# First attention on full-height operands, its maxima sent by DMA, and inputs loaded in two parts

## The chip, the cores and the metric

One NeuronCore of a Trainium2 chip runs the whole program. TensorE (PE) multiplies matrices into PSUM, VectorE (DVE), ScalarE (ACT) and GpSimd (POOL) do the elementwise work, SyncE (SP) issues the DMA transfers. The engines run in parallel, each in its own program order, and wait for each other by semaphores. The metric is the device time of one execution in microseconds (us).

## The reference

A two-layer transformer decoder over 32 sequences of 128 tokens, width 128. Each layer has a cross attention (queries from the layer-normed x, keys and values from a context) and a mixture-of-experts feed-forward block, each added to x. The changed part is the attention of layer 0, with 16 heads of 8 dimensions:

```python
qh = (q @ Wq.T + bq).reshape(B, S, H, Hd).transpose(0, 2, 1, 3)   # H = 16, Hd = 8, S = 128
kh = (k @ Wk.T + bk).reshape(B, S, H, Hd).transpose(0, 2, 1, 3)
vh = (v @ Wv.T + bv).reshape(B, S, H, Hd).transpose(0, 2, 1, 3)
attn = jax.nn.softmax(jnp.einsum('bhqd,bhkd->bhqk', qh, kh) / jnp.sqrt(jnp.float32(Hd)), axis=-1)
out = jnp.einsum('bhqk,bhkd->bhqd', attn, vh)
return out.transpose(0, 2, 1, 3).reshape(B, S, D) @ Wo.T + bo
```

## The kernel before

The program is a sequence of blocks with a barrier between them: loading of the inputs (L1401 to L1427), of a selection constant (L1388 to L1397), of the layer-0 weights (`layer0_weights`, L963), then the attention of layer 0 (`attention0`, L599), the feed-forward block of layer 0 (`ffn`, L1005), the attention of layer 1 (`attention`, L68, with heads of 64 dimensions) and its feed-forward block.

`attention0` handles the 32 sequences in 8 groups of 4. A group's projections are five fills of one PSUM bank (`F_BANK`): x transposed, context transposed, queries, keys, values. Each fill goes PE, ACT (upper part), DVE (the remainder, "lower part"), and the next fill waits for that DVE instruction. Precision is kept by splitting each number into an upper and a lower f16 part. A head's scores need four products over 8 dimensions (upper and lower of q times upper and lower of k), so its operands are laid out over 32 partitions: SP writes the split q and k to a scratch tensor in DRAM (L645) and reads them back spread out (L652, four transfers of 32 partitions each for q and four for k). Partition block 32i to 32i+31 then holds head i of four, and the index r of 0 to 3 selects one of four such sets.

The loop runs over steps s = -11 to 67. A sequence b has two steps, 2b and 2b+1, each with 8 heads. In step s PE does, in this order (L752 to L769): `scores(s)`; `values(s-2)` if s is odd; the transpose of the row maxima of sequence (s+LM0-2)/2 if s is even; `maxima(s+LM0)`; the output projection of sequence (s-4)/2 if s is even; a fill; `values(s-2)` if s is even; the transpose of the attention result if s is odd. LM0 is 4. `maxima` multiplies q by k once so that DVE can take each row's maximum (L856). The maxima, negated, are transposed (L693), copied by ACT (L814), and added into the scores by a second matmul with a selection matrix (L671). So `scores` is 8 matmuls of q and k (L667) and 8 of the selection (L671), each on 32 of the 128 rows of the array and 128 columns long, issued as pairs in two different row blocks. `maxima` is 8 such matmuls (L685). ACT then takes the exponential twice, once to f32 and once to f16 (L807, L808), POOL subtracts the two for the lower part (L916), and `values` is 24 matmuls, 9 columns each (L709 to L711).

What waits for what around the change: `maxima` of a group's first step waits for its q and k transfers (L679); `scores` waits for the copied maxima (L660) and for the exponentials two steps back; the exponentials wait for POOL two steps back; `values` waits for POOL and, at a sequence's first step, for the addition into x (L702). In the fill of group g the steps are 8g-11 to 8g-7.

Of the kernel before, what the change touches and what calls it, by code (L numbers as in the profile page):

```python
# [8 lines left out]
F32 = mybir.dt.float32  # L9
F32R = mybir.dt.float32r  # L10
F16 = mybir.dt.float16
# [5 lines left out]
P = 128  # L17
# [565 lines left out]
LM0 = 4  # L583
RING0 = 4


def fill_of(s):

    g, at = divmod(s + 11, 8)
    if at < 5 and 0 <= g < G:  # L590
        return g, at
    return None


def fills_before(s):
    return sum(1 for t in range(-11, s) if fill_of(t))


def attention0(nc, mem, psum, x_all, ctx_all, const, w, dram):  # L599

    NP = 2 * B
    FIRST, LAST = -11, NP + 4
# [9 lines left out]
    ident, sel = const["ident"], const["sel0"]  # L612
# [6 lines left out]
    q_x, k_x = sb("q_x", [P, 2, 4, 512], F16), sb("k_x", [P, 2, 4, 512], F16)  # L619
    v_hi, v_lo = sb("v_hi", [P, 2, GB, H, D0 + 1], F16), sb("v_lo", [P, 2, GB, H, D0 + 1], F16)  # L620
    negmax, negmax_t = sb("negmax", [P, 2, P]), sb("negmax_t", [P, 2, P], F16)
# [3 lines left out]

    T_BANK, M_BANK, PV, F_BANK = psum[:, 0:4, :], psum[:, 4:6, :], psum[:, 6, :], psum[:, 7, :]
# [4 lines left out]
    s_spill, s_spread = sem("spill"), sem("spread")  # L631
# [4 lines left out]
    with nc.Block() as block:  # L636

        @block.sync
        def _(sp):
            for g in range(G):  # L640
                for m, (hl, wide) in enumerate(((q_hl, q_x), (k_hl, k_x))):
                    sp.wait_ge(s_lo, 5 * g + 3 + m)
                    if g:
                        sp.wait_ge(s_spread, 128 * g)
                    sp.dma_start(dram[m, g % 2], hl[:, :, :]).then_inc(s_spill, 16)  # L645
                    sp.wait_ge(s_spill, 32 * g + 16 * m + 16)
                    if g >= 2:
                        sp.wait_ge(s_sc, 8 * (g - 2) + 8)
                    for t in range(4):
                        part = t // 2 if m == 0 else t % 2  # L650
                        src = dram[m, g % 2].rearrange("(r p) l n -> l p r n", p=32)[part]
                        sp.dma_start(wide[t::4, g % 2, :, :], src).then_inc(s_spread, 16)  # L652

        @block.tensor
        def _(pe):
            def scores(s):
                b, j = divmod(s, 2)
                tok = slice(b % GB * P, (b % GB + 1) * P)
                par = b // GB % 2
# [3 lines left out]
                for r in range(4):  # L663
                    for i in (2 * j, 2 * j + 1):
                        rows = slice(32 * i, 32 * i + 32)
                        o = T_BANK[:, 2 * (s % 2) + i % 2, r * P:(r + 1) * P]
                        nc.tensor.matmul(o, k_x[rows, par, r, tok], q_x[rows, par, r, tok], start=True, stop=False)  # L667
                    for i in (2 * j, 2 * j + 1):
                        rows = slice(32 * i, 32 * i + 32)
                        o = T_BANK[:, 2 * (s % 2) + i % 2, r * P:(r + 1) * P]  # L670
                        last_ = nc.tensor.matmul(o, sel[rows, r, :], negmax_t[rows, b % 2, :], start=False, stop=True)  # L671
                last_.then_inc(s_sc, 1)

            def maxima(s):
                b, j = divmod(s, 2)
                tok = slice(b % GB * P, (b % GB + 1) * P)
                par = b // GB % 2
# [4 lines left out]
                for r in range(4):  # L682
                    for i in (2 * j, 2 * j + 1):
                        rows = slice(32 * i, 32 * i + 32)
                        last_ = nc.tensor.matmul(M_BANK[:, i % 2, r * P:(r + 1) * P], q_x[rows, par, r, tok],  # L685
                                                 k_x[rows, par, r, tok], start=True, stop=True)
                last_.then_inc(s_mm, 1)

            def transpose_maxima(b, s):
                pe.wait_ge(s_max, 2 * b + 2)  # L690
                if n := fills_before(s):
                    pe.wait_ge(s_lo, n)
                nc.tensor.transpose(F_BANK[:, 0:P], negmax[:, b % 2, :], ident[:]).then_inc(s_nmt_mm, 1)  # L693

            def values(s):
                b, j = divmod(s, 2)
                par = b // GB % 2
# [5 lines left out]
                for r in range(4):  # L703
                    for i in (2 * j, 2 * j + 1):
                        h = 4 * r + i
                        o = PV[:, h * (D0 + 1):(h + 1) * (D0 + 1)]
                        q = slice((4 * (i % 2) + r) * P, (4 * (i % 2) + r + 1) * P)
# [15 lines left out]
            def fill(s):  # L723
# [7 lines left out]
                if kind == 0:  # L731
                    pe.wait_ge(s_xhat, g + 1)
                if kind < 2:
# [38 lines left out]
        def _(act):  # L772
            def fill(s):
# [5 lines left out]
                elif kind < 4:  # L779
                    if g:  # L780
                        act.wait_ge(s_spill, 32 * (g - 1) + 16 * (kind - 1))
                    m = kind - 2
                    nc.scalar.activation((q_hl, k_hl)[m][:, 0, :], F_BANK, ACT.Identity,
                                         bias=w["bias"][:, m:m + 1]).then_inc(s_hi, 1)
                else:
                    if g >= 2:
                        act.wait_ge(s_pv, 8 * (g - 2) + 8)
                    nc.scalar.activation(v_hi[:, g % 2, :, :, 0:D0].rearrange("p j h d -> p (j h) d"),
# [3 lines left out]
            for s in range(FIRST, LAST):  # L792
# [16 lines left out]
                if even and 0 <= s + LM0 - 2 < NP:  # L809
                    b = (s + LM0 - 2) // 2  # L810
                    act.wait_ge(s_nmt_mm, b + 1)
                    if b >= 2:
                        act.wait_ge(s_sc, 2 * b - 2)
                    nc.scalar.activation(negmax_t[:, b % 2, :], F_BANK[:, 0:P], ACT.Copy, bias=lifted).then_inc(s_nmt, 1)  # L814
# [4 lines left out]
        def _(dve):  # L819
            def statistics(g):  # L820
                for t in range(GB):
# [9 lines left out]
            def lower(s):  # L831
# [11 lines left out]
                else:  # L843
                    last_ = nc.vector.tensor_tensor(
                        v_lo[:, g % 2, :, :, 0:D0].rearrange("p j h d -> p (j h) d"),
                        F_BANK.rearrange("p (h d) -> p h d", d=D0),
                        v_hi[:, g % 2, :, :, 0:D0].rearrange("p j h d -> p (j h) d"), ALU.subtract)
                last_.then_inc(s_lo, 1)

            def maxima(s):  # L850
                b, j = divmod(s, 2)
                dve.wait_ge(s_mm, s + 1)
                if j == 0 and b >= 2:
                    dve.wait_ge(s_nmt_mm, b - 1)
                out = negmax[:, b % 2, 64 * j:64 * j + 64].rearrange("p (i n) -> p i n", n=32)[:, :, 0:4]
                nc.vector.tensor_reduce(out, M_BANK.rearrange("p i (r k) -> p i r k", k=P), AX.X, ALU.max,  # L856
                                        negate=True).then_inc(s_max, 1)
# [17 lines left out]
            nc.vector.memset(negmax[:, :, :], 0.0)  # L875
# [4 lines left out]
            for s in range(FIRST, LAST):  # L880
# [9 lines left out]
                if s % 8 == 2 and (s + 14) // 8 < G:  # L890
                    statistics((s + 14) // 8)

        @block.gpsimd
        def _(pool):
# [14 lines left out]

            normal(0)  # L910
            for s in range(FIRST, LAST):
                if s % 8 == 3 and (s + 13) // 8 < G:
                    normal((s + 13) // 8)
# [49 lines left out]
def layer0_weights(nc, mem, bank, const, d, w, raw):  # L963


    s_raw, s_mm, s_hi, s_lo = (mem.enter_context(nc.semaphore(n)) for n in ("raw_in", "turned", "split_hi", "split_lo"))
    with nc.Block() as block:

        @block.sync
        def _(sp):  # L970
            for n in ("wq", "wk", "wv", "wo", "gate", "bv", "bo"):
                sp.dma_start(raw[n], d[n]).then_inc(s_raw, 16)
            sp.dma_start(w["bias"][:, 0:1], d["bq"]).then_inc(s_raw, 16)
            sp.dma_start(w["bias"][:, 1:2], d["bk"]).then_inc(s_raw, 16)
            sp.wait_ge(s_raw, 16 * 9)
# [583 lines left out]
```

## Time and profile before

| | us |
|---|---|
| median of 3 runs | 1698.66 (1693.28 to 1699.65) |
| the profiled execution | 1695.49 |
| its span, first to last instruction | 1693.7 |
| first scores of layer 0 to its last exponentials | 71.1 to 335.4 |
| PE busy over the span | 1401.0 (83%) |
| DVE, ACT, POOL busy | 949.1, 814.0, 661.4 |

The profile lists instructions with start and duration. "L685" is line 685 of the kernel. PE is the matmul, PEld the load of its stationary operand, SPq the issue of a DMA by SP. A bracket such as [6.15 <-DMA k_x_a<-spill] says how long the engine had been idle and what released it. PEclk is the granted TensorE clock as a share of 2.4 GHz.

### The profile page before, as it was taken

To read this page: it belongs to the slowest core of one execution; us is meant where nothing else is said; L and a number is where in the kernel's file an instruction comes from. 1 tells how busy PE (TensorE), PEld (TensorE's weight loads), DVE (VectorE), ACT (ScalarE), POOL (GpSimd) and SP (SyncE) were. 2 spreads that over 40 slices of the span, in tenths; PEclk is the share of its full clock that TensorE was granted. 3 is DMA by queue.
4 is the path that set the end of the run, shared out by engine and by line. 5 is a ranking of instruction groups with operands and counts; after the bars stand their busy time and mean duration, and the time that the engine had idled before them with its cause. 6 is when DMAs were issued, how large, how long until landed. Compare 5 with 4: busy or idle time off the path is not lost. (4 is left out here: it accounts for less than half of the span.)

```text
span 1693.7 us, 31779 instructions
## 1 busy us (share of the span) xinstructions
PE 1401.0 (83%) x11720; PEld 1123.0 (66%) x11720; DVE 949.1 (56%) x2066; ACT 814.0 (48%) x1335; POOL 661.4 (39%) x556
## 2 busy tenths in 40 slices
PE   0599999806599999999993798988988989836698
PEld 0477777606488888888882477777777777736486
DVE  0455544337656665666563666665666666527665
ACT  0255655521344444444442465655656556521354
POOL 1266656602155555555552123333232332412254
PEclk9999655555799999999996899998999899965799
DMA  4211111040000000000001000000000000010000
GB/s 114 75 39 39 46 63 45 2 149 1 1 1 1 1 1 1 0 0 0 0 0 62 1 2 1 2 1 3 2 1 3 2 1 2 2 32 1 1 25 25
DMA packets 27575, 31.59 MB, mean 19 GB/s; under 512 B 4721, under 2 KB 21682, under 8 KB 27314
## 3 DMA queue, kind: packets, MB, share of 16 engines
q1 hardware_dynamic: 27442, 29.75, 5.7%
q8 instruction: 91, 1.49, 0.4%
q14 instruction: 42, 0.34, 0.1%
HBM read 23.45 MB, written 6.29 MB: 18 GB/s over the span
## 5 line engine op out<-in xcount | busy, mean ns | idle before, releaser
L1347 POOL TENSOR_TENSOR w_lo_f<-weighted_f,w_hi_f 128x512 fp32r<-128x512 f32 x232 | 300.6, 1296 | 345.8 <-ACT w_hi_f L1289 345.8
L565 POOL TENSOR_TENSOR p_lo_l<-probs_l,p_hi_l 128x512 f16<-128x512 f32 x128 | 148.2, 1158 | 336.5 <-ACT p_hi_l L358 336.5
L1327 DVE TENSOR_TENSOR hidden_f<-psum,gate_act_f 128x512 f32<-128x512 f32 x232 | 160.5, 692 | 210.0 <-PE psum L1239 199.3
L1304 ACT ACTIVATE gate_act_f<-psum 128x512 f32<-128x512 f32 x232 | 138.7, 598 | 269.0 <-PE psum L1239 267.6
L916 POOL TENSOR_TENSOR p_lo_a<-probs_a,p_hi_a 128x1024 f16<-128x1024 f32 x64 | 135.9, 2127 | 112.9 <-ACT p_hi_a L808 112.9
L1333 DVE TENSOR_TENSOR weighted_f<-psum,hidden_f 128x512 f32<-128x512 f32 x232 | 160.5, 692 | 9.0
L1239 PE MATMUL psum<-x_lo_f,w_hi 128*128 (+1 forms) x384 | 153.8, 401 | 0.0
L1237 PE MATMUL psum<-x_hi_f,w_hi 128*128 (+1 forms) x384 | 152.0, 396 | 1.8 <-PEq L1135 1.8
L1238 PE MATMUL psum<-x_hi_f,w_lo 128*128 (+1 forms) x384 | 151.8, 395 | 0.0
L1289 ACT ACTIVATE w_hi_f<-weighted_f 128x512 fp32r<-128x512 f32 x232 | 144.9, 625 | 2.2 <-DVE weighted_f L1333 2.2
L356 ACT ACTIVATE probs_l<-psum,lift_l 128x512 f32<-128x512 f32 x128 | 88.0, 688 | 105.0 <-PE psum L232 105.0
L228 PE MATMUL psum<-q_a_l,k_a_l 64*128 64x128 f16 x512 | 115.9, 226 | 19.2 <-ACT negmax_t_l L350 11.8
L232 PE MATMUL psum<-negmax_t_l,sel 64*128 64x128 f16 x512 | 115.4, 225 | 0.0
L230 PE MATMUL psum<-q_a_l,k_b_l 64*128 64x128 f16 x512 | 115.4, 225 | 0.0
L229 PE MATMUL psum<-q_b_l,k_a_l 64*128 64x128 f16 x512 | 115.4, 225 | 0.0
L856 DVE TENSOR_REDUCE negmax_a<-psum 128x8 f32<-128x1024 f32 x64 | 78.3, 1224 | 42.6 <-PE psum L685 42.6
L807 ACT ACTIVATE probs_a<-psum 128x1024 f32<-128x1024 f32 x64 | 65.5, 1023 | 68.9 <-PE psum L671 68.9
L1243 PE MATMUL psum<-comb_t_f,pick 128*128 (+1 forms) x232 | 92.2, 397 | 0.0
L459 DVE TENSOR_REDUCE negmax_l<-psum 128x4 f32<-128x512 f32 x128 | 87.0, 682 | 1.6 <-PE psum L202 1.3
L358 ACT ACTIVATE p_hi_l<-psum,lift_l 128x512 f16<-128x512 f32 x128 | 87.0, 679 | 0.0
L1237 PEld LDWEIGHTS psum<-x_hi_f,w_hi 128*128 128x128 f32 x384 | 73.3, 191 | 19.1 <-issue 2.2
L1238 PEld LDWEIGHTS psum<-x_hi_f,w_lo 128*128 128x128 f32 x384 | 72.6, 189 | 17.4
(257 smaller groups left out, 3797.9 us busy)
## 6 DMA issues: line engine op xcount, KB each, us to landing
q_x_a<-spill SPq DMA_DIRECT2D x32, 128.0 KB, 2.6
k_x_a<-spill SPq DMA_DIRECT2D x32, 128.0 KB, 2.5
spill<-q_hl_a SPq DMA_DIRECT2D x8, 256.0 KB, 2.0
spill<-k_hl_a SPq DMA_DIRECT2D x8, 256.0 KB, 2.9
out<-x_all SPq DMA_DIRECT2D x8, 256.0 KB, 2.3
pick_raw<-c_pick SPq DMA_DIRECT2D x1, 1536.0 KB, 6.2
stage<-L_ffn_w SPq DMA_DIRECT2D x3, 256.0 KB, 3.0
stage<-L_xattn_Wq SPq DMA_DIRECT2D x1, 512.0 KB, 3.5
```

Of the source, the lines that this page charges most:

```text
L228: nc.tensor.matmul(o, ka, qa, start=True, stop=False)
L229: nc.tensor.matmul(o, ka, q_b[rows, parity, ch, tok], start=False, stop=False)
L565: nc.gpsimd.tensor_tensor(p_lo[:, r, :], probs[:, r, :], p_hi[:, r, :], ALU.subtract).then_inc(s_exp_lo, 1)
L916: nc.gpsimd.tensor_tensor(p_lo[:, s % RING0, :], probs[:, s % 2, :], p_hi[:, s % RING0, :], ALU.subtract).then_inc(s_plo, 1)
L1237: nc.tensor.matmul(dst[:, :], hi[:, a], x1, start=True, stop=False)
L1238: nc.tensor.matmul(dst[:, :], lo[:, a], x1, start=False, stop=False)
L1239: nc.tensor.matmul(dst[:, :], hi[:, a], x2, start=False, stop=True).then_inc(done, 1)
L1289: nc.scalar.activation(w_hi[:, slot, :], weighted[:, (parity * nc_ + k) % 2, :], ACT.Copy).then_inc(s_wh, 1)
L1304: nc.scalar.activation(gate_act[:, slot, :], GATE[slot][:, :], ACT.Silu).then_inc(s_silu, 1)
L1327: nc.vector.tensor_tensor(hidden[:, slot, :], UP[slot][:, :], gate_act[:, slot, :], ALU.mult).then_inc(s_hid, 1)
L1333: nc.vector.tensor_tensor(weighted[:, slot, :], CB[slot][:, :], hidden[:, slot, :], ALU.mult).then_inc(s_a, 1)
L1347: nc.gpsimd.tensor_tensor(w_lo[:, slot, :], weighted[:, (parity * nc_ + k) % 2, :], w_hi[:, slot, :].bitcast(F32), ALU.subtract).then_inc( ...
```

## The change

Operands of `attention0` now take all 128 rows of the array. q is spread into `q_pad`, where head i of a set has data only in partitions 32i to 32i+31 of its own 512 columns and zeros elsewhere, so one matmul of 128 rows and 512 columns gives four heads (`scores`: 2 matmuls a step in place of 16), and `maxima` is 8 matmuls of 128 rows. Partition 3 of k holds ones, and partition 3 of q the negated maxima of the sequence, written by one more DMA per sequence (`maxima_row`); the selection constant, its block and its matmuls go. The q transfers are eight of 16 partitions and one that clears partition 3; the k transfers are three of 32 partitions and one of 31. There are three buffers in place of two, LM0 is 6, the fills of group g are at steps 8g-14 to 8g-10, and `scores` waits for the DMA of the maxima. DVE and POOL set `q_pad` and `k_x` at the start of the attention block. SP follows the step order. The opening loads the first group's rows of x, the weights and the first group's rows of the context first, and the other rows last, in the same block; the statistics and the context transpose of group 1 wait for them.

```diff
-LM0 = 4
+LM0 = 6
+FILL0 = 14
+NB0 = 3
+SPREADS = 13
@@ SP
-            for g in range(G):
-                for m, (hl, wide) in enumerate(((q_hl, q_x), (k_hl, k_x))):
-                    sp.wait_ge(s_lo, 5 * g + 3 + m)
...
-                    for t in range(4):
-                        sp.dma_start(wide[t::4, g % 2, :, :], src).then_inc(s_spread, 16)
+            def spread_queries(g):
+                sp.wait_ge(s_spill_q, 16 * g + 16)
+                if g >= NB0:
+                    sp.wait_ge(s_sc, 8 * (g - NB0) + 8)
+                halves = narrow_q[g % 2].rearrange("(r i d) l n -> i (d l) r n", r=4, i=4)
+                for i in range(4):
+                    for t in range(2):
+                        sp.dma_start(q_pad[32 * i + t:32 * i + 32:2, g % NB0, :, i, :], halves[i]).then_inc(s_spread, 16)
+                others = q_pad[3:4, g % NB0, :, 1:4, :].rearrange("o r i n -> o r (i n)")
+                sp.dma_start(others, nothing[:, :].unsqueeze(1).broadcast_to([1, 4, 1536])).then_inc(s_spread, 16)
+            def spread_keys(g):
+                sp.wait_ge(s_spill_k, 16 * g + 16)
+                halves = narrow_k[g % 2].rearrange("(r p) l n -> l p r n", p=32)
+                for t in range(4):
+                    skip = int(t == 3)
+                    sp.dma_start(k_x[t + 4 * skip::4, g % NB0, :, :], halves[t % 2, skip:32]).then_inc(s_spread, 16)
+            def maxima_row(b):
+                sp.wait_ge(s_nmt, b + 1)
+                tok = slice(b % GB * P, (b % GB + 1) * P)
+                dst = q_pad[3:4, b // GB % NB0, :, :, tok].rearrange("o r i n -> o (r i) n")
+                sp.dma_start(dst, negmax_t[:, b % 4, :]).then_inc(s_row[b % 4], 16)
+            sp.wait_ge(s_clear, 3)
+            for s in range(FIRST, LAST):
+                if s % 2 == 0 and 0 <= s + LM0 - 2 < NP:
+                    maxima_row((s + LM0 - 2) // 2)
+                g, at = divmod(s + FILL0, 8)
+                if at == 3 and 0 <= g < G:
+                    spill_queries(g)
+                if at == 4 and 0 <= g < G:
+                    spill_keys(g)
+                if at == 5 and 0 <= g < G:
+                    spread_queries(g)
+                if at == 6 and 0 <= g < G:
+                    spread_keys(g)
@@ PE, scores
-                pe.wait_ge(s_nmt, b + 1)
+                pe.wait_ge(s_row[b % 4], 16 * (b // 4 + 1))
...
+                for r in (2 * j, 2 * j + 1):
+                    last_ = nc.tensor.matmul(T_BANK[:, 2 * (s % 2) + r % 2, :], k_x[:, par, r, tok], q_pad[:, par, r, :, tok],
+                                             start=True, stop=True)
@@ PE, maxima
-                    pe.wait_ge(s_spread, 128 * (s // 8) + 128)
+                    pe.wait_ge(s_spread, SPREADS * 16 * (s // 8 + 1))
...
+                for r in (2 * j, 2 * j + 1):
+                    for i in range(4):
+                        last_ = nc.tensor.matmul(M_BANK[:, r % 2, i * P:(i + 1) * P], q_pad[:, par, r, i, tok],
+                                                 k_x[:, par, r, tok], start=True, stop=True)
@@ DVE and POOL, at the start of the block
-            nc.vector.memset(negmax[:, :, :], 0.0)
+            nc.vector.memset(nothing[:, :], 0.0)
+            nc.vector.memset(k_x[:, :, :, :], 1.0)
+            nc.vector.memset(q_pad[:, 0, :, :, :], 0.0).then_inc(s_clear, 1)
...
+            nc.gpsimd.memset(q_pad[:, 1, :, :, :], 0.0).then_inc(s_clear, 1)
+            nc.gpsimd.memset(q_pad[:, 2, :, :, :], 0.0).then_inc(s_clear, 1)
@@ the opening block
+                sp.dma_start(rows(x_all, 0, GB), x_rows[:, 0:GB, :]).then_inc(s_in, 16)
...
+                    sp.dma_start(dst, src).then_inc(s_raw, 16)
+                for dst, src in ((rows(ctx_all, 0, GB), ctx_rows[:, 0:GB, :]), (maskt[:, :], a["mask_BxS2_fk1"]),
...
+                sp.dma_start(rows(x_all, GB, B), x_rows[:, GB:B, :]).then_inc(const["s_rest"], 16)
+                sp.dma_start(rows(ctx_all, GB, B), ctx_rows[:, GB:B, :]).then_inc(const["s_rest"], 16)
```

## Rows read from the trace of the kernel before

**Rows 1.** Stretches: us, busy time and count per engine, PEclk, DMA share.
```profile
71.00:107.00 36.00, 32.14 (x407) 24.47 (x406) 17.87 (x31) 22.71 (x32) 21.41 (x15) 1.00 0.16 53
182.50:247.20 64.70, 60.29 (x788) 46.30 (x788) 32.44 (x63) 37.54 (x55) 41.81 (x28) 0.50 0.12 39
1180.00:1500.00 320.00, 291.64 (x3331) 238.95 (x3331) 194.84 (x474) 190.36 (x321) 98.46 (x96) 0.94 0.01 2
```

**Rows 2.** PE in order of time, layer 0: start, us, line, shape, count.
```profile
62.92 0.61 PE L685 MATMUL psum<-k_x_a,q_x_a 32*128 32x128 f16 x8 [1.32 <-DVE negmax_a L856]
...
177.88 0.63 PE L741 MATMUL psum<-c_lo_a,wk_hi 128*128 128x512 f32 x1
178.31 0.63 PE L742 MATMUL psum<-c_hi_a,wk_lo 128*128 128x512 f32 x1
...
180.74 0.40 PE L685 MATMUL psum<-k_x_a,q_x_a 32*128 32x128 f16 x8
```

**Rows 3.** ACT in order of time: exponentials of steps 0, 16, 24, 32, 54, 56, 63.
```profile
72.17 1.02 ACT L807 ACTIVATE probs_a<-psum 128x1024 f32<-128x1024 f32 x1 [0.28 <-PE psum L671]
...
139.95 1.02 ACT L807 ACTIVATE probs_a<-psum 128x1024 f32<-128x1024 f32 x1 [0.33 <-PE psum L671]
175.06 1.02 ACT L807 ACTIVATE probs_a<-psum 128x1024 f32<-128x1024 f32 x1 [0.33 <-PE psum L671]
208.30 1.02 ACT L807 ACTIVATE probs_a<-psum 128x1024 f32<-128x1024 f32 x1 [0.33 <-PE psum L671]
...
302.18 1.02 ACT L807 ACTIVATE probs_a<-psum 128x1024 f32<-128x1024 f32 x1 [0.69 <-PE psum L671]
309.37 1.02 ACT L807 ACTIVATE probs_a<-psum 128x1024 f32<-128x1024 f32 x1 [0.70 <-PE psum L671]
333.44 1.02 ACT L807 ACTIVATE probs_a<-psum 128x1024 f32<-128x1024 f32 x1 [1.43 <-PE psum L671]
```

**Rows 4.** PE in order of time, one step's scores in layer 0.
```profile
305.84 0.32 PE L667 MATMUL psum<-q_x_a,k_x_a 32*128 32x128 f16 x2
305.94 0.32 PE L671 MATMUL psum<-negmax_t_a,sel 32*128 32x128 f16 x2
```

**Rows 5.** PE in order of time, scores in layer 1.
```profile
1018.05 0.22 PE L228 MATMUL psum<-q_a_l,k_a_l 64*128 64x128 f16 x1
1018.10 0.22 PE L229 MATMUL psum<-q_b_l,k_a_l 64*128 64x128 f16 x1
```

**Rows 6.** SP's key transfers, then the DMA view of 182 to 190 us.
```profile
183.28 2.53 SPq L652 DMA_DIRECT2D k_x_a<-spill  x4
...
q1 hardware_dynamic: 651, 0.64, 24.6%
...
k_x_a<-spill SPq DMA_DIRECT2D x4, 128.0 KB, 2.6
```

**Rows 7.** The opening and the first group, in order of time.
```profile
4.29 4.74 SPq L1411 DMA_DIRECT2D ctx_all<-ctx  x1
...
20.80 0.36 SPq L1392 DMA_DIRECT2D sel_raw<-c_sel  x1
...
29.87 0.48 PE L983 MATMUL psum<-ident,raw_wq 128*128 128x128 f32 x1 [9.55 <-DMA bias<-L_xattn_bk]
...
33.08 0.27 DVE L875 MEMSET negmax_a<- 128x256 f32 x1 [0.39 <-PEq L967]
...
40.47 1.12 PE L736 MATMUL psum<-ident,xhat_a 128*128 128x128 f32 x4 [8.09 <-POOL xhat_a L906]
...
51.21 0.75 DVE L841 SCALAR_TENSOR_TENSOR k_hl_a<-psum,bias,k_hl_a 128x512 f16<-128x512 f32 x1 [2.46 <-ACT k_hl_a L783]
...
60.99 0.61 PE L685 MATMUL psum<-k_x_a,q_x_a 32*128 32x128 f16 x8 [6.15 <-DMA k_x_a<-spill]
```

**Rows 8.** Groups by line: xcount, busy us, mean ns, idle before.
```profile
L1150 DVE MEMSET comb_t_f<- 32x4096 f32 x2 | 6.9, 3472 | 1.8 <-issue 1.8
L916 POOL TENSOR_TENSOR p_lo_a<-probs_a,p_hi_a 128x1024 f16<-128x1024 f32 x63 | 133.8, 2127 | 111.7 <-ACT p_hi_a L808 111.6
```

More of the change, by code:

```diff
@@ L595, in fills_before @@
 def fills_before(s):
-    return sum(1 for t in range(-11, s) if fill_of(t))
+    return sum(1 for t in range(-FILL0, s) if fill_of(t))
 def attention0(nc, mem, psum, x_all, ctx_all, const, w, dram):
     NP = 2 * B
-    FIRST, LAST = -11, NP + 4
+    FIRST, LAST = -FILL0, NP + 4
     scale = float(np.float32(1.0) / np.sqrt(np.float32(D0)))
@@ L630, in attention0 @@
     s_fill, s_hi, s_lo = sem("fill"), sem("hi"), sem("lo")
-    s_spill, s_spread = sem("spill"), sem("spread")
+    s_spill_q, s_spill_k, s_spread = sem("spill_q"), sem("spill_k"), sem("spread")
+    s_row = [sem(f"row_{n}") for n in range(4)]
+    s_clear = sem("clear")
     s_mm, s_max, s_nmt_mm, s_nmt = sem("max_mm"), sem("max"), sem("nmt_mm"), sem("nmt")
@@ L658, in scores @@
                 tok = slice(b % GB * P, (b % GB + 1) * P)
-                par = b // GB % 2
-                pe.wait_ge(s_nmt, b + 1)
+                par = b // GB % NB0
+                pe.wait_ge(s_row[b % 4], 16 * (b // 4 + 1))
                 if s >= 2:
                     pe.wait_ge(s_exp_hi, s - 1)
[L663 to L671, printed above, removed]
+                for r in (2 * j, 2 * j + 1):
+                    last_ = nc.tensor.matmul(T_BANK[:, 2 * (s % 2) + r % 2, :], k_x[:, par, r, tok], q_pad[:, par, r, :, tok],
+                                             start=True, stop=True)
                 last_.then_inc(s_sc, 1)
@@ L676, in maxima @@
                 tok = slice(b % GB * P, (b % GB + 1) * P)
-                par = b // GB % 2
+                par = b // GB % NB0
                 if s % 8 == 0:
-                    pe.wait_ge(s_spread, 128 * (s // 8) + 128)
+                    pe.wait_ge(s_spread, SPREADS * 16 * (s // 8 + 1))
                 if s >= 1:
                     pe.wait_ge(s_max, s)
[L682 to L686, printed above, removed]
+                for r in (2 * j, 2 * j + 1):
+                    for i in range(4):
+                        last_ = nc.tensor.matmul(M_BANK[:, r % 2, i * P:(i + 1) * P], q_pad[:, par, r, i, tok],
+                                                 k_x[:, par, r, tok], start=True, stop=True)
                 last_.then_inc(s_mm, 1)
@@ L732, in fill @@
                     pe.wait_ge(s_xhat, g + 1)
+                if kind == 1 and g == 1:
+                    pe.wait_ge(const["s_rest"], 32)
                 if kind < 2:
@@ L889, in _ @@
                     lower(s)
-                if s % 8 == 2 and (s + 14) // 8 < G:
-                    statistics((s + 14) // 8)
+                if s % 8 == 7 and (s + 17) // 8 < G:
+                    statistics((s + 17) // 8)
         @block.gpsimd
@@ L1524, in constants @@
     rows = np.arange(P)
-    sel0 = np.zeros((P, 4, P), f)
     sel1 = np.zeros((P, 8, P), f)
-    for m in range(4):
-        sel0[rows % 32 == m, m, :] = 1
     for m in range(8):
@@ L1554 @@
     out = nc.dram_tensor("out", (B, S, D), F32, kind="ExternalOutput").ap()
[L1555 removed]
+    spill = (nc.dram_tensor("narrow_q", (2, P, 2, 512), F16, kind="Internal").ap(),
+             nc.dram_tensor("narrow_k", (2, P, 2, 512), F16, kind="Internal").ap())
     program(nc, args, out, spill)
```

135 lines of the change are left out of this document (62 added, 73 removed).

## The prediction

> **What bounds the kernel now.** I read the stretches first. The change touches the first 335 us, so only the layer-0 attention and the opening matter. In its loop PE is busy 32.1 of 36 us and 60.3 of 64.7 us, while DVE, ACT and POOL are at about half to two thirds [rows 1]. PE sets the pace. Its clock comes next: PEclk is 0.50 in 182.5 to 247.2 us, the lower level (1.2 GHz). Up to about 179 us the column prints 1.00, but the instructions contradict it: eight maxima matmuls took 0.61 us at 62.9, and 0.40 at 180.7, in a short stretch that began right after two 512-column projections on all 128 rows [rows 2]. So the loop runs at 1.2 GHz nearly throughout. Layer 1's attention, on 64 rows and with wider fills, has 0.94 granted, which is the full level for 88% of its time [rows 1].
>
> The exponentials give the pace. Step 0 to step 63 lasts 72.17 to 333.44, 261.3 us. A pair of steps without a fill takes 309.37 - 302.18 = 7.19 us, so eight steps 28.8. Eight steps with fills take 175.06 - 139.95 = 35.1, so five fills add 6.3. The next eight, with the short stretch at full clock, took 33.2: about 3.4 us of full clock saved 1.9 us [rows 3].
>
> **The change in the loop.** At the low clock `scores` costs what it did. Now a pair of 32-row matmuls starts every 0.10 to 0.11 us, eight pairs are 0.85 us [rows 4]. Then two matmuls of 512 columns follow at 0.43 us (178.31 - 177.88), 0.86 [rows 2]. The selection matmuls were half of the pairs, and this is what pays for the lost pairing. `maxima` loses its pairing without such a saving: four starts of 0.107 become eight, +0.42 a step, +0.85 a pair. Of that 0.25 lies under DVE's normalisation, for which PE waits at the end of an odd step. So a pair goes from 7.19 to 7.8, eight steps to 31.2, with fills 37.5.
>
> At the full clock a 128-column matmul starts every 0.05 to 0.056 us [rows 5], and what streams halves: scores -0.86 a pair, maxima -0.8, projection and the two transposes -0.6 together (estimates from the same halving). `values` is bound by its 24 loads of the stationary operand and stays, as do the waits for DVE. A pair takes 5.6, eight steps 22.4, with fills (6.3 becomes 4) 26.4. As a check, this is a ratio of 1.4, and the stretch above ran 5.3 us of work in 3.4, 1.55. POOL needs 21.4 us in 36 us of the loop, ACT 22.7 [rows 1]; 22.4 to 26.4 lies just above, so these are the next bound.
>
> How much of the loop gets the full clock no row shows. The ends are none, as now, and 88% as in layer 1. Nearest is layer 1, since both now stream mostly over the array's height, but here PE stops twice a pair for DVE. I take two thirds. Rates then mix: with fills 1/(0.667/26.4 + 0.333/37.5) = 29.3, without 24.7. Fills of groups 2 to 7 lie in steps 0 to 47: 6 x 29.3 + 24.7 + (24.7 x 7/8 - 3 for six steps without maxima) = 219 us.
>
> The moved wait is `maxima` of a group's first step, now at step 8g-6, for 13 transfers. In front of it on SP, from the start T of step 8g-10: the copied maxima are ready at T+2.9, one row (0.5) and the spill of k (0.5), nine q transfers (at least 0.4 each with half the descriptors, at most 0.64; 4.4), the row of step 8g-8 at T+9.1, four k transfers in 2.53 [rows 6]. The last is issued at T+11.1 and lands 2.6 later [rows 6], T+13.7. PE comes to it at T+12.8 (four steps of 2.95, scores, a transpose). That is a wait of 1 us, seven times, 7. Behind it on PE stand the projection, the fill and `values`, so ACT and POOL run dry too, and nothing hides it. The rows of maxima themselves are issued four steps ahead of their use, over 11 us against some 3, and cost nothing even if one is held up by the q transfers. Loop: 219 + 7 - 261.3 = -35.3.
>
> The k transfer of 31 partitions has no row. If it goes like one of 32 it lands in 2.6. If its 31 x 4 pieces of 1 KB go one after another: 651 packets took 24.6% of 16 x 8 us, 48 ns each [rows 6], so 124 take 6.0 in place of 0.4, and it lands 5.6 later. The nearest row is that of 32 partitions; I take it in the sum, and the other end is a rival. On this the Trainium skill has a rule ("DMA: Bandwidth & Descriptors", section "Why a DMA increments its semaphore by 16 and not by 1"): a transfer runs on the largest number of engines up to 16 that divides its slowest dimension on both sides. By it 31 rows go to one engine, and the sum would be the rival's below. No row of this trace shows such a shape.
>
> **The opening.** SP ends the last issue at 9.03 (4.29 + 4.74). The new order puts eleven small issues of about 0.46 before it, so the block ends at about 14.4 rather than 20.8; the selection block (20.80 to 24) and the wait of the weights block (to 29.87) go, its work (29.87 to 33.08) and a barrier stay. The attention block starts at 18.0, not 33.1 [rows 7]. There the memsets stand ahead of the statistics: DVE has 1536 + 6144 + 8192 elements at 0.85 ns (3472 ns for 4096) [rows 8], 13.4 us. POOL has two of 8192, without a row: at DVE's rate 13.9, at 2.08 ns (2127 for 1024, two inputs) [rows 8] 34.1. I take 13.9, one output and no input being nearer to a memset; it runs beside DVE's and ends before the statistics do. With the 7.4 us from 33.08 to 40.47 and the dropped 0.3, the first transposes start at 38.5: -2.0 of the 15 that the loads give. The late rows of x and context are in SBUF before group 1 asks; if not, their wait is again behind the first group's keys. The Trainium skill ("VectorE: DVE Perf Modes", "Zero memsets can be issued as uint32 (trn2)") would halve the zero fill of `q_pad`, 3.5 us less on DVE; the 16-bit memsets of this trace are too small to tell.
>
> **The first group.** From its transposes to its first maxima now 60.99 - 40.47 = 20.5 [rows 7]; nine q transfers in front of the keys, instead of four, add 0.7, since the keys are spilled only after 51.96. From there to the first exponential 11.2 us now, with two steps of fills. With LM0 = 6 all five fills of group 1 come first: four of them lasted 40.47 to 51.96, 11.5, the fifth some 4, then two transposes and the last step, 2.2, and the row's DMA, 1: 18.7, +7.5. Sum +8.2.
>
> **Sum.** -35.3 - 2.0 + 8.2 = -29. The profiled execution took 1695.49 (span 1693.7 and 1.8 around it), 0.2% under the median of 1698.66; from it, 1666.
>
> **Rivals.** (a) The keys' last transfer goes piece by piece, and a wait takes the place of the pace. 5.6 us at each of the seven group changes and once in the first group: +45, 1711, slower than before. For it: 31 has no divisor. Against it: the step lengths hide it in part if the loop is slower than I think. It decides from 3.6 us of lateness on (8 x 3.6 = 29, the whole gain), and from 4.7 the loss is one that can be measured (29 and 8.5). (b) The clock stays at 1.2 GHz. Loop 6 x 37.5 + 31.2 + 24.3 = 280.5, four steps last longer than the transfers, so no wait: +19.2 - 2.0 + 8.2 = +25, 1721. For it: PE busy at 93% did not raise it so far [rows 1]. Against: the only rises in the loop came after full-height work. (c) The loop gains, but POOL fills its buffers at the higher price: transposes at 56.6 in place of 38.5, +18, 1684. (d) The change of operands doesn't pay at all because POOL and ACT take over as bound: that is the 22.4 of the forecast, it can't cost more.
>
> **How the numbers follow.** Forecast 0.42, (a) 0.33, (b) 0.15, (c) 0.10. Low end: full clock all the time, 6 x 26.4 + 22.4 + 16.6 = 197, no wait, halved zero fills: 1695.5 - 64 + 8.2 - 2.0 - 3.5 = 1634; high end: most of (b), 1720. The forecast's own range is 1634 to 1690. What a measurement can tell here is 0.5%, 8.5 us. Faster: 0.38 of the forecast's 0.42, 0.02 of (a), 0.05 of (c), 0.45. Slower: 0.24 of (a), 0.13 of (b), 0.01 of (c), 0.38. The rest, 0.17, is no change.
>
> **What would show it.** Right: PEclk at 1.00 in most of the loop, with eight maxima in under 0.7 us; an exponential pair every 5.6 us without fills; PE idle before a group's first maxima, released by `k_x`, about 1 us. The first transposes start near 38.5, the first exponential near 78. Wrong by (a): that wait is over 5 us and recurs in each group, and the 31-row transfer lands some 8 us after its issue. By (b): PEclk 0.50 and a pair at 7.8. By (c): POOL's memsets over 10 us each. The forecast fails altogether if SP's queue holds up the rows of maxima so that `scores` waits at every sequence.

## The result, and the profile after

The changed kernel takes 1708.75 us (median of 4 runs, 1707.64 to 1708.9), the kernel before 1697.94 beside it. The ratio is 1.0067, with a 95% interval of 1.0046 to 1.0087: slower by 0.7%. The interval lies above 1, but its lower end is just under the 0.5% that the prediction took as the least a measurement can tell from no change. The forecast was 1666, faster.

The stretches come first, as [rows 1] did. Columns as there.

```profile
71.00:107.00 36.00, 23.34 (x169) 16.68 (x169) 16.05 (x25) 13.98 (x21) 13.59 (x11) 0.62 0.14 45
182.50:247.20 64.70, 43.18 (x626) 33.27 (x627) 31.54 (x64) 34.94 (x53) 40.21 (x27) 0.82 0.15 47
1190.00:1510.00 320.00, 291.73 (x3339) 239.35 (x3336) 196.33 (x480) 191.15 (x322) 100.51 (x100) 0.94 0.01 2
```

The second row shows the odd thing about this result. PE's granted clock rose from 0.50 to 0.82, PE is busy 43.2 us of 64.7 instead of 60.3, and DVE, ACT and POOL do about as much in the stretch as before (31.5, 34.9 and 40.2 us against 32.4, 37.5 and 41.8). So the engine that set the pace got its relief, and the pace stayed. What took its place stands in the waits of PE between 60 and 360 us (total, how many, the longest):

```profile
PE psum L719 <- DMA k_x_a<-narrow_k: 62.0, 8, 13.5
PE psum L745 <- DVE x_all L914: 13.3, 13, 1.4
```

L719 are the maxima, and the wait is the moved one, for a group's key transfers. Before there was one such wait, of 6.2 us, the one in the last row of [rows 7]. Now there are eight: 13.5 us in the first group and 48.5 in the seven changes of group, 6.9 each on average. Over the whole loop PE is busy for 174.8 us of 260.8, against 241.4 of 261.3 before. This is the change to group 4, SP's queue first and then PE:

```profile
189.65 0.70 SPq L666 DMA_DIRECT2D q_pad_a<-nothing_a  x1
190.40 0.57 SPq L679 DMA_DIRECT2D q_pad_a<-negmax_t_a  x1
191.02 3.11 SPq L673 DMA_DIRECT2D k_x_a<-narrow_k  x4
```

```profile
191.71 1.01 PE L719 MATMUL psum<-k_x_a,q_pad_a 128*128 128x128 f16 x8
192.80 1.06 PE L705 MATMUL psum<-q_pad_a,k_x_a 128*128 128x512 f16 x2
194.04 0.38 PE L729 MATMUL psum<-ident,negmax_a 128*16 128x128 f32 x1 [0.18 <-DVE negmax_a L897]
201.44 1.04 PE L719 MATMUL psum<-k_x_a,q_pad_a 128*128 128x128 f16 x8 [7.02 <-DMA k_x_a<-narrow_k]
203.23 1.06 PE L774 MATMUL psum<-ident,xhat_a 128*128 128x128 f32 x4
204.77 0.59 PE L705 MATMUL psum<-q_pad_a,k_x_a 128*128 128x512 f16 x2
205.81 0.61 PE L719 MATMUL psum<-k_x_a,q_pad_a 128*128 128x128 f16 x8
```

SP has issued the last key transfer at 194.13 and PE gets on at 201.44, 7.3 us later; [rows 6] have 2.6 from issue to landing for one of 32 partitions. The view by stretches for the same gap says how the data travels:

```profile
195.50:201.20 5.70, 0.00 (x0) 0.00 (x0) 0.00 (x0) 2.08 (x3) 4.53 (x3) 0.50 0.07 21
```

A DMA share of 0.07 is what one engine of sixteen would give (1/16 = 0.06), and the data moves at 21 GB/s. The last transfer, 31 partitions of 4 KB, is 127 thousand bytes; at that rate it takes 6.0 us, the 6.0 that rival (a) had worked out from packets. The L705 and L719 rows of this gap also show the two levels of the clock: two 512-column matmuls take 1.06 or 0.59 us, eight of 128 columns 1.04 or 0.61.

The opening and the first group, against [rows 7] and the memset of [rows 8]:

```profile
9.49 4.51 SPq L1446 DMA_DIRECT2D ctx_all<-ctx  x1
...
18.25 0.70 DVE L916 MEMSET nothing_a<- 1x768 uint32 x1 [0.48 <-PEq L1012]
20.18 5.18 DVE L917 MEMSET k_x_a<- 128x6144 f16 x1 [1.23 <-issue]
26.16 3.47 DVE L918 MEMSET q_pad_a<- 128x4096 uint32 x1 [0.80 <-issue]
31.35 0.87 DVE L864 BATCH_NORM_STATS2 stats_a<-x_all 128x6 f32<-128x128 f32 x4
...
18.03 6.92 POOL L953 MEMSET q_pad_a<- 128x8192 f16 x1 [17.60 <-POOLq L1012]
24.89 6.93 POOL L954 MEMSET q_pad_a<- 128x8192 f16 x1
...
37.32 1.12 PE L774 MATMUL psum<-ident,xhat_a 128*128 128x128 f32 x4 [19.87 <-POOL xhat_a L949]
...
49.23 5.16 SPq L664 DMA_DIRECT2D q_pad_a<-narrow_q  x8
54.43 0.71 SPq L666 DMA_DIRECT2D q_pad_a<-nothing_a  x1
55.19 2.68 SPq L673 DMA_DIRECT2D k_x_a<-narrow_k  x4
...
65.20 1.03 PE L719 MATMUL psum<-k_x_a,q_pad_a 128*128 128x128 f16 x8 [13.51 <-DMA k_x_a<-narrow_k]
```

SP has issued the late rows by 14.0 us, the selection block and the wait behind it are gone, and the attention block starts at 18.0. Then DVE's statistics wait for its memsets until 31.35, and the first transposes for the statistics. In the last row PE has waited 13.51 us for the keys, 7.3 of them after SP's last issue ended at 57.87.

And the exponentials of steps 0, 16, 24 and 32, as in [rows 3]; the last is at 343.97:

```profile
83.20 1.02 ACT L847 ACTIVATE probs_a<-psum 128x1024 f32<-128x1024 f32 x1 [1.13 <-PE psum L705]
...
152.94 1.02 ACT L847 ACTIVATE probs_a<-psum 128x1024 f32<-128x1024 f32 x1
187.10 1.02 ACT L847 ACTIVATE probs_a<-psum 128x1024 f32<-128x1024 f32 x1
221.66 1.02 ACT L847 ACTIVATE probs_a<-psum 128x1024 f32<-128x1024 f32 x1
```

Eight steps take 34.2 and 34.6 us, each with a wait of about 7 for keys in it, against 35.1 and 33.2 before.

Where the 13.0 us of the spans (1706.7 - 1693.7) come from, in four parts:

| | before | after | difference | forecast |
|---|---|---|---|---|
| to the first transposes | 40.47 | 37.32 | -3.2 | -2.0 |
| from there to the first exponential | 31.7 | 45.9 | +14.2 | +8.2 |
| first to last exponential (the loop) | 261.3 | 260.8 | -0.5 | -35.3 |
| the rest of the span | 1360.3 | 1362.7 | +2.5 | 0 |

### The profile page after: what moved, and what is told of

It is laid out like the page before. It is cut to its first block and busy times, and to the rows that moved or that the text cites. A ratio compares the mean times of both kernels' runs of the same rounds, so it can differ in the third digit from the quotient of the medians.

```text
span 1706.7 us, 30035 instructions
## 1 busy us (share of the span) xinstructions
PE 1338.4 (78%) x10824; PEld 1072.0 (63%) x10824; DVE 956.2 (56%) x2068; ACT 808.2 (47%) x1334; POOL 675.7 (40%) x558
## 5 line engine op out<-in xcount | busy, mean ns | idle before, releaser
L719 PE MATMUL psum<-k_x_a,q_pad_a 128*128 128x128 f16 x512 | 48.5, 251 | 62.9 <-DMA k_x_a<-narrow_k 62.0
```

## The experiments

"Theory" is that the key transfer of 31 partitions goes over one DMA engine and turns the gain into a wait. All times are medians; the kernel before is 1697.5 to 1699.3 in the comparisons. "Loop" is first to last exponential, always of the one profiled execution, and so are the waits and the clock.

**e1_split: the last key transfer of the changed kernel in two pieces.**

```diff
-                for t in range(4):
-                    skip = int(t == 3)
-                    sp.dma_start(k_x[t + 4 * skip::4, ...], halves[t % 2, skip:32])
+                for t in range(3):
+                    sp.dma_start(k_x[t::4, ...], halves[t % 2])
+                sp.dma_start(k_x[7:68:4, ...], halves[1, 1:17])      # 16 partitions
+                sp.dma_start(k_x[71::4, ...], halves[1, 17:32])      # 15 partitions
```

> The changed kernel with the key transfer of 31 partitions cut into one of 16 and one of 15, nothing else. Theory (the 31-partition transfer goes piece by piece and is what PE waits for): it lands about 2.6 us after its issue like its neighbours, the wait before a group's first maxima falls from about 7 us to 1 or 2 and in the first group by about 5, so 35 to 45 us less than the changed kernel, 1664 to 1674. Rival (SP's long order, 13 issues and the rows of maxima between, makes every key transfer late): one more issue in that order, so the same or up to 5 us slower, 1709 to 1714.

Measured: 1675.67, ratio 0.9874 (0.9858 to 0.9891). One more DMA in each group, the same bytes, and the kernel is 33 us faster than the changed one. The first group and the waits of PE:

```profile
57.15 0.60 SPq L673 DMA_DIRECT2D k_x_a<-narrow_k  x1
57.80 0.92 SPq L674 DMA_DIRECT2D k_x_a<-narrow_k  x1
...
60.23 1.04 PE L720 MATMUL psum<-k_x_a,q_pad_a 128*128 128x128 f16 x8 [8.58 <-DMA k_x_a<-narrow_k]
```

```profile
PE psum L720 <- DMA k_x_a<-narrow_k: 23.8, 8, 8.6
```

The last piece lands 2.4 us after its issue begins. The waits of PE for keys fall by 38.2 us (62.0 - 23.8), the span by 35.8 (1706.7 - 1670.9). The first exponential is at 77.31 and the loop 232.5 us.

**e2_first: the 31-partition transfer is issued first of the four, not last.**

```diff
-                for t in range(4):
+                for t in (3, 0, 1, 2):
```

> The changed kernel with the 31-partition key transfer issued first of the four instead of last. Theory (piece by piece, some 8 us from issue to landing): it starts three issues or about 1.9 us earlier and the others land before it, so each of the eight waits shortens by 1.9 us: 15 us less, 1694. Rival (all key transfers are late by SP's order): their last landing is where it was, no change, 1709.

Measured: 1699.52, ratio 1.0004 (0.9985 to 1.0022): 9 us less than the changed kernel, between the theory's 15 and the rival's none. The wait in the first group is 12.3 us, all eight are 50.5. An earlier start takes 1.4 us off each wait ((62.0 - 50.5) / 8), and what stays is still twice the 23.8 of e1_split. So the length of this transfer is the main cause, and its place at the end of the queue a small part of the wait.

**e5_before31: the kernel before, its last key transfer as 1 + 31 partitions.**

```diff
-                        sp.dma_start(wide[t::4, g % 2, :, :], src).then_inc(s_spread, 16)
+                        if m == 1 and t == 3:      # keys, last transfer
+                            sp.dma_start(wide[3:4, ...], src[0:1])
+                            sp.dma_start(wide[7::4, ...], src[1:32])
+                        else: ...                  # as before
```

> The kernel before with its last key transfer (32 partitions) issued as one of 1 and one of 31 partitions. It measures the shape by itself. Theory (31 rows go piece by piece): the transfer of 31 lands about 8 us after its issue, the first group starts 6 us later, and in the loop, where PE comes 4 us after the landing (191.8 against 187.8), 2 us of each of seven are seen: 1698 + 6 + 15 = 1719, and at least 1708. Rival (31 rows spread like 32): one issue more, 1698 to 1700.

Measured: 1713.03, ratio 1.009 (1.0074 to 1.0107). The old kernel, with its 32-row tiles, loses through this alone as much as the change did (1.009 against 1.0067; the intervals overlap):

```profile
58.83 0.68 SPq L654 DMA_DIRECT2D k_x_a<-spill  x1
...
66.66 0.60 PE L689 MATMUL psum<-k_x_a,q_x_a 32*128 32x128 f16 x8 [11.80 <-DMA k_x_a<-spill]
```

Issue to use is 7.8 us. This is the price by itself, away from the rest of the change. It shows as a first exponential 5.7 us later (77.84) and as waits of 6.2 us in five of the seven changes of group, 1.2 each instead of the 2 in all seven that were expected. The loop grows by 9.7 us (271.0). The other 3.5 are about what two groups of the kernel before had saved by a stretch at the full clock (33.2 and 33.3 us instead of 35.1 for eight steps); here no eight steps take less than 35.1 up to step 48, and PE is busy for 4.0 us more with the same work (245.4 against 241.4).

**e7_before30: the same with 2 + 30 partitions.** The edit is that of e5_before31 with the cut after two rows.

> The kernel before, its last key transfer (32 partitions of 4 KB) issued as 2 and 30 partitions instead of one; e5_before31 did this with 1 and 31, which made its 31-partition transfer land 7.8 us after issue and the kernel 1713. Theory (the pieces of a transfer go over as many engines as divide its partitions' count, and 31 has no divisor in reach but 1): 30 has 15, so it lands about 3 us after issue, and the time is 1697 to 1702. Rival (any count of partitions that isn't a multiple of 16 is slow, or two issues in place of one are what cost): landing 6 us or more after issue, as in e5_before31, time 1708 to 1714.

Measured: 1699.31, ratio 1.0004 (0.9989 to 1.0019).

```profile
59.08 0.92 SPq L654 DMA_DIRECT2D k_x_a<-spill  x1
...
62.06 0.60 PE L689 MATMUL psum<-k_x_a,q_x_a 32*128 32x128 f16 x8 [6.96 <-DMA k_x_a<-spill]
```

30 partitions are in use 3.0 us after the issue began, 31 after 7.8. Two issues in place of one cost nothing that can be measured. That the count isn't a multiple of 16 costs nothing either. 31 is slow; it has no divisor between 2 and 16, while 30 has 15.

**e4_opening: the kernel before with the new opening only.** The opening's issues, its waits and the weights block are those of the change (see its diff); the layer-0 attention and the selection block stay.

> The kernel before with the new opening alone (first group's rows and weights first, the rest late; the selection constant's block stays). Theory (the loads give their whole gain where no memsets stand behind them): the attention block starts at 14.4 + 3.2 + 3.5 = 21.3 rather than 33.1, all that follows moves with it, 12 us less than before, 1686. Rival (the late rows of x and context hold up group 1, or the first group waits for its transfers): under 5 us gained.

Measured: 1694.06, ratio 0.9982 (0.9969 to 0.9995), 3 us less instead of the theory's 12. The first exponential is at 67.21, 5.0 us earlier than before. The rest of what the opening could give went here, and neither of the rival's two reasons was it:

```profile
14.47 5.63 SPq L1388 DMA_DIRECT2D sel_raw<-c_sel  x1
...
24.52 0.63 ACT L1393 ACTIVATE sel<-sel_raw 128x512 f16<-128x512 f32 x1 [8.77 <-DMA sel_raw<-c_sel]
```

The selection's small load stands behind the late rows of x and context: its issue takes 5.63 us instead of 0.36 [rows 7], and ACT and the weights behind it wait. In the full change this load is gone. In the profiled execution (1696.53, the slowest of the ten) the loop is 3.6 us longer (264.9 against 261.3): from step 8 to 48 every eight steps take 35.1 us, whereas before two of the five groups had a stretch at the full clock and took 33.2 and 33.3. This isn't shown to be an effect of the opening, since it differs between executions of one kernel. PEclk prints 1.00 throughout this loop, though its eight maxima matmuls take 0.60 us, the time of the lower level; the mean clock of the execution then prints as 0.94. Of the 19 executions of the kernel before that ran beside this one, six print 0.94; their median is 1699.9 us, that of the other 13 is 1696.85.

**e6_early: e1_split with the large memsets in the opening block.**

```diff
+            # opening block; q_pad, k_x and nothing are allocated there
+            nc.vector.memset(nothing[:, :], 0.0)
+            nc.vector.memset(k_x[:, :, :, :], 1.0)
+            nc.vector.memset(q_pad[:, 0, :, :, :], 0.0)
+            nc.gpsimd.memset(q_pad[:, 1, :, :, :], 0.0)
+            nc.gpsimd.memset(q_pad[:, 2, :, :, :], 0.0)
```

> The changed kernel with the last key transfer cut into 16 and 15 partitions (e1_split), and its large memsets (the ones of k_x, the zeros of q_pad, the clear row's zeros) moved from the head of layer 0 into the opening block, where VectorE and GpSimd wait for the first transfers. Theory (the head of layer 0 is the memsets: statistics on VectorE start at 31.4 behind them, and the first transposes at 37.3): the first transposes come at 24 to 27 us, the first exponential 10 to 12 us earlier than in e1_split (77.3), at 65 to 67, and the time is 1663 to 1666. Rival (the transposes' other need, the weights and the rest of the rows, or the key transfers behind a busy queue, comes just behind): the first exponential only 2 to 5 us earlier, time 1671 to 1674.

Measured: 1666.87, ratio 0.9814 (0.9798 to 0.9831); 8.8 us less than e1_split by the medians, 5.9 by the two profiled spans.

```profile
9.31 3.47 DVE L1461 MEMSET q_pad_a<- 128x4096 uint32 x1 [0.80 <-issue]
...
25.99 1.12 PE L772 MATMUL psum<-ident,xhat_a 128*128 128x128 f32 x4 [8.39 <-POOL xhat_a L944]
```

The first transposes come 11.3 us earlier, the first exponential 10.2 (67.1). So in the changed kernel the memsets, not the loads, ended the opening.

**e9_ahead: e6_early with a group's projections and transfers one step earlier.**

```diff
-FILL0 = 14
+FILL0 = 15
```

> e6_early with the projections, spills and spreads of a group one step earlier in the order (15 steps ahead of the first use of a group instead of 14). Theory (the 2.2 us that e1_split still waits at each of seven changes of group is a transfer that lands a little late, not a queue that is full): the key waits at the group changes go to nothing, 7 times 2.2 = 15 us less in the loop and as much less time than e6_early if the granted clock stays as it is, 10 to 15 us. Rival (TensorE then waits for the next thing, VectorE's maxima or the exponentials, or the clock falls): the key waits go but the loop gets under 5 us shorter. Second rival: the projections now stand on the steps of the maxima's transposes and share their bank, and the step gets longer: same as e6_early or slower.

Measured: 1663.31, ratio 0.98 (0.9768 to 0.9832), the fastest kernel of the study. But it is only 3.6 us under e6_early, and the intervals overlap. The waits of PE from 40 to 330 us, in which e6_early has 23.9 us for the keys:

```profile
PE psum L743 <- DVE x_all L912: 18.2, 21, 1.4
PE psum L772 <- POOL xhat_a L944: 15.3, 7, 7.3
...
PE psum L717 <- DMA k_x_a<-narrow_k: 0.2, 1, 0.2
```

The key waits are gone. In their place PE waits longer for the residual sum (18.2 instead of 12.9 us) and for the next group's normalised rows: 15.3 us, of which 7.3 stand before the loop, at the first projection of group 1, and 8 are new in the loop. The loop is 230.6 us, 3.8 shorter. PE is idle for 7.3 us less in it (47.9 against 55.3), but the same instructions keep it busy for 3.6 us more (182.7 against 179.1), with a mean granted clock of 0.78 in place of 0.80. The theory of a late transfer holds, its price does not: the first rival, that the next wait steps in or the clock falls, is the better account.

**e3_extra: the kernel before with two idle full-height matmuls a step.** What was left open is the clock: 0.50 before, 0.82 after.

```diff
             def scores(s):
                 ...
+                for r in (0, 1):
+                    nc.tensor.matmul(T_BANK[:, 2 * (s % 2) + r, :], k_x[:, par, r, tok], q_x[:, par, r, :], ...)
                 for r in range(4):
```

> The kernel before, its maxima and scores still in 32-row tiles, with two more matmuls in every step of layer 0: all 128 rows of k_x against 512 columns, into the bank that the step's scores then overwrite. They do no needed work (64 steps of two). Theory (the granted clock in layer 0 rises because full-height matmuls take the place of those in 32-row tiles, not because the work is less): the loop's granted clock rises from 0.50 to 0.7 or more somewhere in its length, and the added 0.86 us a step at 1.2 GHz is paid back by all of TensorE's work going faster: loop 225 to 262 us, time 1665 to 1700. Rival (the clock is set by something else, such as the order of the transfers or how long TensorE waits): the granted clock stays 0.50, the step grows from 4.15 to about 5.0 us, the loop from 261 to about 315, and the time is about 1750. Below nothing added (loop under 261 with more work done) only the theory is left.

Measured: 1737.68, ratio 1.0236 (1.0209 to 1.0263). In stretches of 40 us:

```profile
150.00:190.00 40.00, 38.52 (x435) 26.08 (x434) 16.70 (x32) 19.56 (x28) 20.35 (x14) 0.50 0.13 41
...
230.00:270.00 40.00, 36.64 (x472) 24.51 (x471) 19.05 (x35) 21.36 (x32) 23.41 (x15) 0.67 0.13 41
```

Neither side had it. The clock stays at its lower level most of the time, the loop grows by 42.3 us (303.6), and the theory's 1665 to 1700 is refuted for this addition. Where it rose (0.67) eight steps took 36.8 instead of 41.7 us, so the rival's 1750 is missed too.

**e11_more: the same addition, to the kernel whose matmuls are all full height (e6_early).**

```diff
+                    nc.tensor.matmul(T_BANK[:, 2 * (s % 2) + r % 2, :], q_pad[:, par, r, 0, tok], k_x[:, par, r, :], ...)
                     last_ = nc.tensor.matmul(T_BANK[:, 2 * (s % 2) + r % 2, :], k_x[...], q_pad[...], ...)
```

> e6_early with two more matmuls in every step of layer 0: q_pad on all 128 rows against 512 columns of k_x, into the bank that the step's scores then overwrite; no needed work. It is e3_extra's addition, made to the kernel in which all matmuls of the loop are full height. Theory left after e3_extra (the clock comes with the share of the loop's time in which TensorE streams columns over the whole array; e3_extra added too little to a loop whose other half stayed in 32-row tiles): the granted clock of the loop, 0.74 to 0.87 in e6_early, rises to 0.95 or more, the added work is paid for in part, and the loop (234.3 us) grows by 0 to 15: time 1665 to 1682. Rival (more work means no better clock; what counts is something else, such as its pauses): the granted clock stays at 0.75 to 0.87, each step grows by 0.43 to 0.86 us, the loop by 27 to 40: time 1694 to 1707.

Measured: 1670.58, ratio 0.9825 (0.9807 to 0.9844). One stretch of e6_early, then the same of e11_more:

```profile
150.00:190.00 40.00, 31.68 (x428) 23.66 (x425) 23.55 (x44) 26.74 (x41) 25.93 (x17) 0.87 0.19 60
```

```profile
150.00:190.00 40.00, 33.68 (x462) 24.15 (x459) 22.43 (x41) 25.34 (x39) 26.16 (x17) 0.96 0.18 56
```

The added work is 64 x 0.43 = 27.5 us at the full clock; the loop grows by 5.1 (239.5). But PE's idle time in the loop fell too, from 55.3 to 46.7 us, of which 4.0 are key waits, so a part of this is cover for waits and not the clock. (The next expectation puts that fall at 24 to 11; the 11 leaves out the first group's wait.)

**e12_both and e13_half: the addition (two or one a step) on e9_ahead, which has no key waits.**

> e9_ahead with e11_more's addition: two more full-height matmuls of 512 columns in every step of layer 0, no needed work. In e11_more the granted clock rose from 0.67 to 0.87 (stretches of 40 us) to 0.84 to 0.96 and the loop grew by 5 us for 27 us of added work. Theory (the clock is carried by full-height streaming, and pauses at group changes bring it down): with no key waits the clock is 0.95 or more throughout, the loop 225 to 236 us (e9_ahead 230.6), time 1656 to 1668. Rival (the gain of e11_more was the key waits that its longer steps covered, 24 us in e6_early and 11 in e11_more, not the clock): without waits to cover, the added work shows, loop 245 or more, time 1677 or more.

> As e12_both with one added matmul a step instead of two: 13.7 us of added work at the full clock. Theory: the clock lies between e9_ahead's (0.76 to 0.90) and e12_both's, the loop at or below e9_ahead's 230.6, time 1653 to 1664. Rival: each added matmul costs its time, loop 237 or more, time 1670 or more.

Measured: e12_both 1665.95, ratio 0.9829 (0.9795 to 0.9864), loop 231.9; e13_half 1666.56, ratio 0.9806 (0.9786 to 0.9827), loop 237.8. e9_ahead first, then e12_both:

```profile
230.00:270.00 40.00, 32.38 (x450) 24.33 (x451) 20.14 (x32) 25.26 (x38) 25.10 (x12) 0.80 0.14 42
```

```profile
230.00:270.00 40.00, 31.39 (x454) 22.46 (x451) 20.78 (x33) 26.17 (x39) 25.56 (x15) 1.00 0.16 48
```

With no key waits to cover, 27.5 us of work that nobody needs costs 1.3 us in the loop (2.6 by the medians). It doesn't go into the other waits either: PE's idle time in the loop doesn't fall (49.9 us against 47.9), and PE is busy no longer with 127 matmuls more (182.0 against 182.7), because nearly all else on it runs at the full level (mean clock 0.96 against 0.78). That is the clock's own worth. As a change it brings nothing: neither kernel is faster than e9_ahead. e13_half misses the theory's 1653 to 1664 by 2.6 us; its profiled execution is the slowest of its four (1671.06), with a loop as the rival had it, and its clock lies between (0.88 to 0.91 from 110 to 270 us), as the theory had it. How one added matmul a step divides between cost and gain stays open.

## Why the prediction was wrong

**The step that failed** is the landing of the keys' last transfer: "The nearest row is that of 32 partitions; I take it in the sum". It was taken as 2.6 us and is 7.8 (e5_before31). It was seen, priced and left as rival (a), with a chance of 0.33. The prediction's own working had both ends, and no row of the trace chose between them. The row nearest in size was the wrong one: 30 partitions take 3.0 us and 31 take 7.8, so what counts is not the number of partitions but what divides it. Here the Trainium skill had the answer, "DMA: Bandwidth & Descriptors", section "Why a DMA increments its semaphore by 16 and not by 1": a transfer uses the largest number of engines, up to 16, that divides its slowest dimension on both sides. The runs agree with it in all cases tried: 31 partitions take 7.8 us, at one engine's share in the changed kernel, 30 partitions 3.0, and 16 + 15 partitions 2.4. A rule that names the shape at hand should have outweighed a row with another shape.

**The price of (a)** was 5.6 us in each of eight places, 45 together. The 5.6 held: in the first group of the changed kernel the keys are in use at 65.20, some 8.0 us after the last issue began (about 57.2), in e1_split 2.4. The split begins its last issue 0.6 us later, though, so each of its waits is shorter by 4.8 us on average, 38.2 together, and the time by 33; a late start of a group is given back in part behind the wait. That the 1711 of rival (a) lies only 2 us from the measured 1708.75 is in part luck: its 45 was 12 more than the split gave back, and the 1666 that it was added to was 10 too low.

**The rest of the sum** is tested by e1_split, the kernel that the forecast described.

- The clock: "I take two thirds". In e1_split the granted clock from 90 to 290 us is 0.81, 0.91, 0.84, 0.73 and 0.79 in stretches of 40 us, a mean of 0.82, which is the full level for 63% of the time. Right, as a choice that no row had supported.
- The loop: 232.5 us, 217.3 without the seven waits, against 226 and 219. The rate was right; the wait was 8 us too short. It counted 4.4 us for the nine q issues and 2.5 for the keys'; in e1_split's first group they took 5.9 and 3.5 (five issues for the keys). And PE's way to the wait was reckoned with steps of 2.95 us, which has no source; the prediction's own rate without fills, 24.7 / 8 = 3.09, would have left a wait of 0.3 and not 1.
- The two rates: a pair of steps without fills was to take 5.6 us at the full clock and 7.8 at the lower one. In e6_early a pair at PEclk 1.00 takes 5.74 us (275.15 to 280.89), and the one pair at 0.50 takes 7.31 (267.84 to 275.15). The first is right to 0.2, the second was 0.5 too dear, as far as one pair can tell.
- The opening: the attention block's start at 18.0 was right to 0.1, the first transposes at 37.3 instead of 38.5. The large fill of `q_pad` on DVE took 3.47 us instead of 7, since it runs as 4096 uint32, as the Trainium skill says in "VectorE: DVE Perf Modes", section "Zero memsets can be issued as uint32 (trn2)". Gaps of 0.5 to 1.2 us ahead of each memset, with no price in the sum, took that back: the statistics start at 31.35, the 18.0 + 13.4 of the forecast. The 1.2 us came from the old block's small memsets, 33.08 to 34.5, of which the sum dropped only 0.3.
- The first group: +8.2 forecast, +8.3 in e1_split (77.31 - 37.28 = 40.0 against 31.7), +14.2 in the changed kernel with the slow transfer. The sum is right in part by luck: up to the first maxima e1_split takes 22.9 us (60.23 - 37.28) and not 21.2, from there to the first exponential 17.1 and not 18.7.
- Rivals (b), (c) and (d): the clock did rise; POOL's memsets took 6.92 us, the 13.9 for two that the sum had; ACT and POOL aren't the bound at 35 and 40 of 64.7 us.

So with a transfer that lands as assumed the forecast of 1666 stands against a median of 1675.67. The profiled execution of e1_split, which the parts above describe, took 1672.82. Of its 6.8 us over the forecast 6.5 are the loop: 8.2 of waits, less 1.7 in the rate.

The 2.5 us by which the changed kernel is longer after its last exponential are no effect of the change that can be told: with the same instructions there, this part takes between 1359.5 (e3_extra) and 1363.6 us (e6_early) in the 13 profiled executions.

**Not explained:** what decides the level of the clock. The runs show that full-height work raises it in one kernel and hardly in another that keeps its 32-row tiles (e11_more, e12_both, e3_extra); that the tiles as such hold it down was not separated from the order and the amount of the work. A kernel with tiled maxima and full-height scores would do that; it wasn't tried.

## What to carry to other kernels

Read the count of partitions of every DMA that a wait hangs on: one row taken out of 32 left 31, which only 1 divides up to 16, and the transfer took 7.8 us instead of 2.6, with one engine's share of the DMA; two pieces of 16 and 15 cost 0.9 us more issue time in each group and saved 33 us. When the engine that sets the pace has a quarter less to do (PE busy 174.8 us in the loop instead of 241.4), the transfers that had slack are next: here the loop's gain of 29 us (e1_split) went into seven waits of 6.9, which the busy shares don't show and the list of waits does at once.

## What was not expected of the hardware

- 120 KB of keys on 30 partitions were in use 3.0 us after the issue began, 124 KB on 31 partitions after 7.8. While PE waits for such a transfer in the changed kernel, the DMA share is 0.07.
- A small load that is issued behind a large one costs its issuer: 5.63 instead of 0.36 us on SP (e4_opening).
- Work can be free on PE: 27.5 us of matmuls without a use cost 1.3 us in e12_both, since the granted clock went from 0.80 to 1.00 in 230 to 270 us. In e3_extra two such matmuls a step cost 42.3 us in the loop, with the clock at 0.50 for most of it.
- GpSimd fills 8192 16-bit elements a partition in 6.92 us (0.845 ns each), the rate of VectorE's ones (6144 in 5.18, 0.843 ns).
